# Sorted expert tiles started inside the first stage's tail: 48 of 144 run from a table made at half of the tokens

## What is computed

```python
rw = gating(h2)                                  # [b, t, 16], at most a few experts per token
q = einsum('btc,ech,bte->bth', x2, q_proj, rw)   # k and v alike
attn = softmax(causal(q @ k.T / sqrt(128)))
out = einsum('bth,ehc,bte->btc', attn @ v, o_proj, rw)
return h + attn_linear + out
```

## Time and profile before

| what | value |
|---|---|
| median of 3 runs | 1015.23 us (1014.79 to 1015.39) |
| profiled execution, its own time | 1013.34 us |
| its span | 1011.6 us |
| busy: PE, DVE, ACT, POOL | 928.0, 836.3, 600.6, 632.1 us |
| PE's share of the chain that ended last | 55% (DVE 26%) |
| DMA, mean over the span | 136 GB/s |

### The profile page before, as it was taken

How to read it: one execution, slowest core, us unless ns; L and a number is a source line. 1 busy time by engine, 2 the same in 40 slices (tenths; PEclk the granted TensorE clock), 3 DMA queues, 4 the chain that set the end, 5 groups by cost and what they waited for, 6 DMA issues and landing times.

```text
span 1011.6 us, 20470 instructions
## 1 busy us (share of the span) xinstructions
PE 928.0 (92%) x5230; PEld 800.2 (79%) x5230; DVE 836.3 (83%) x2884; ACT 600.6 (59%) x1633; POOL 632.1 (62%) x832
## 2 busy tenths in 40 slices
PE   4999999999999845999999959999999999999997
PEld 3787788788788734899999938888888888888876
DVE  4789999999999875655555539999999999999998
ACT  4666766666676511644444436666666666666664
POOL 5447777777777678100000058888888888888885
PEclk9999999999999956999999969999999999999999
DMA  2123344443333236898878633333333333333331
GB/s 65 48 74 120 121 142 150 143 146 126 122 125 117 93 109 215 264 298 260 258 248 265 227 116 104 103 104 103 104 104 105 101 105 106 103 105 104 91 105 37
DMA packets 106297, 137.53 MB, mean 136 GB/s; under 512 B 13762, under 2 KB 93634, under 8 KB 106180
## 3 DMA queue, kind: packets, MB, share of 16 engines
q1 hardware_dynamic: 87348, 83.98, 26.7%
q0 software_dynamic: 17408, 50.35, 16.4%
q10 hardware_dynamic: 1424, 1.84, 0.5%
HBM read 70.06 MB, written 66.06 MB: 135 GB/s over the span
## 4 chain that ended last, share of the span: by engine, by line
PE 55%; DVE 26%; POOL 8%; issue 6%; ACT 2%; DMA 2%; SPq 1%; POOLq 0%; DVEq 0%; ACTq 0%
PE bank L1395 15%; PE bank L1396 15%; PE bank L1397 15%; PE bank L1402 5%; DVE phi L1085 4%; DVE attn L1097 2%; DVE kvm L1118 2%; POOL sorted_x L701 2%; DVE stats L1125 2%; POOL row_y L776 2%; DVE stats L970 2%; DVE zden L1094 1%; PE bank L1421 1%; PE bank L1592 1%; PE bank L1598 1%
## 5 line engine op out<-in xcount | busy, mean ns | idle before, releaser
L1395 PE MATMUL bank<-wo_hi,split_lo 128*128 128x512 f32 x512 | 213.7, 417 | 1.5 <-DVE split_lo L1363 1.4
L1396 PE MATMUL bank<-wo_lo,split_hi 128*128 128x512 f32 x512 | 202.8, 396 | 0.0
L1397 PE MATMUL bank<-wo_hi,split_hi 128*128 128x512 f32 x512 | 202.2, 395 | 0.0
L776 POOL DMA_INDIRECT row_y<-sorted_y,pair_now x128 | 131.5, 1027 | 32.1 <-issue 22.9
L769 POOL COPY pair_now<-pair_at 128x2 uint32<-128x2 uint32 x64 | 12.2, 191 | 176.9 <-SPq L574 176.9
L900 ACT ACTIVATE h<-bank,rwo 128x256 f32<-128x256 f32 x256 | 107.2, 472 | 25.0 <-PE bank L1397 15.9
L1234 DVE TENSOR_TENSOR split_lo<-bank,split_hi 128x256 fp32r<-128x256 f32 x144 | 60.8, 422 | 68.6 <-ACT split_hi L861 67.1
L1397 PEld LDWEIGHTS bank<-wo_hi,split_hi 128*128 128x128 f32 x512 | 96.9, 189 | 22.5
L1395 PEld LDWEIGHTS bank<-wo_hi,split_lo 128*128 128x128 f32 x512 | 97.1, 190 | 20.6 <-DVE x L1332 1.6
L1332 DVE SCALAR_TENSOR_TENSOR x<-bank,rwo,x 128x256 f32<-128x256 f32 x256 | 111.1, 474 | 1.1 <-PE bank L1397 1.0
L1332 DVE SCALAR_TENSOR_TENSOR qk_e<-bank,rwo,qk_e 128x256 f32<-128x256 f32 x256 | 110.9, 474 | 0.3 <-PE bank L1397 0.2
(11 more groups left out here) (212 smaller groups left out, 2538.3 us busy)
## 6 DMA issues: line engine op xcount, KB each, us to landing
sorted_y<-row_y SPq DMA_DIRECT2D x36, 384.0 KB, 3.1
sorted_y<-w_attn SPq DMA_DIRECT2D x36, 384.0 KB, 3.2
row_x<-sorted_x SPq DMA_DIRECT2D x72, 128.0 KB, 2.9
h_rows<-h SPq DMA_DIRECT2D x64, 128.0 KB, 1.7
row_x<-h_rows SPq DMA_DIRECT2D x64, 128.0 KB, 3.5
out_h<-row_x SPq DMA_DIRECT2D x64, 128.0 KB, 2.1
phi<-sorted_x SPq DMA_DIRECT2D x36, 128.0 KB, 2.9
qk_neg<-sorted_x SPq DMA_DIRECT2D x36, 128.0 KB, 3.0
```

The costliest lines, as they stand in the source:

```text
L776: pool.indirect_dma_start(out=row_y[:, 2 * tile.p + n, :], out_offset=None, in_=sorted_y, in_offset=offsets(pair_now[tile.q][:, n:n + 1])) ...
L1395: pe.matmul(ps, left[1][c], right[0][c], start=(c == 0), stop=False)
L1396: pe.matmul(ps, left[0][c], right[1][c], start=False, stop=False)
L1397: last = pe.matmul(ps, left[0][c], right[0][c], start=False, stop=(c == n - 1))
```

## The change

The first 48 sorted tiles (`EARLY`) are taken from what is sorted once 32 of the 64 token tiles are ranked. 64 x 128 pairs over 16 experts hold at least 49 full tiles, so 48 full ones are always there. A table of their own (`tab_early`, `early_i`) is formed by DVE in 17 operations, two per step from step 35 on, with a count and two turns by PE added to the rank products. `run1` ends at step 60 for PE, ACT and DVE. Then `run_early` goes through pair tiles -2 to 47; in front of each, `tail(c)` puts the pieces that steps 61 to 67 and the table had. POOL keeps its old steps, and has the late scatters spread otherwise (2, 3, 3, 4, 4, 4, 4 at steps 59, 60, 61, 62, 63, 65, 67, where it had 4, 4, 4, 4, 4, 4 at 59, 60, 61, 63, 65, 67). SP loads tiles 0 to 3 inside the first stage, 4 to 7 behind step 60, and does all 16 fills between tiles 24 and 39. The second table, for the remaining 96 tiles, counts what the first has used. The branch comes behind tile 47.

Buffers: loads of tiles go to `h4` in place of `row_x`; the early tiles' results go to six places (`w_attn` and the raw weight buffers); `ps_y` has three banks in place of four, since one bank holds the tail's products. POOL's shift has 31 pairs of operations, since each expert has two pieces. The pair weights, formed between the tables and the stage before, go in pieces beside tiles 48 to 52, and `routing_part` beside 53 to 57.

```diff
-        ps_turn, ps_y = banks[0:2], banks[2:6]
+        ps_turn, ps_y, ps_dense = banks[0:2], banks[2:5], banks[2:6]
...
+        def run_early(eng, step, tail):
+            for c in range(-2, EARLY):
+                tail(c)
+                step(Tile(c))
...
-            run1(sp, step1)
-            for p in range(2):
-                sp.wait_ge(h2_stored[p], 16 * (B // 2))
-            fill_regions(sp, 0)
-
-            sp.wait_ge(regions_filled, 16 * E)
-            sp.wait_ge(dummies_zeroed, 16 * E)
-            for t in range(B - N_X2, B):
-                scatter_done(sp, t)
+            run1(sp, step1, TAIL_STEP - 3)
+            sp.wait_ge(early_ready, 1)
+            for t in range(EARLY_TOKENS - N_X2, EARLY_TOKENS):
+                scatter_done(sp, t)
+            after(sp, "h2", Tile(B - 5))
+            for c in range(4):
+                load_pair(Tile(c))
+            step1(Tile(TAIL_STEP - 2))
+            step1(Tile(TAIL_STEP - 1))
+            after(sp, "kv_product", Tile(B - 1))
+            after(sp, "qk_exp", Tile(B - 1))
+            for c in range(4, 8):
+                load_pair(Tile(c))
+            step1(Tile(TAIL_STEP))
+
+            for c in range(EARLY):
+                if c == 24:
+                    sp.wait_ge(fill_ready, 1)
+                if 24 <= c < 24 + E:
+                    half, n = divmod(c - 24, E // 2)
+                    if n == 0:
+                        fills.update(enumerate(fill_rows(sp, half)))
+                    sp.dma_start(sorted_x[bass.ds(fills[n], P), :], zeros[:, :]).then_inc(regions_filled, 16)
+                if c + 8 == EARLY:
+                    sp.wait_ge(tables_ready, 1)
+                    sp.wait_ge(regions_filled, 16 * E)
+                    sp.wait_ge(dummies_zeroed, 16 * E)
+                    for t in range(B - N_X2, B):
+                        scatter_done(sp, t)
+                load_pair(Tile(c + 8))
+                if c >= 2 and c % 2 == 0:
+                    store_pair(Tile(c - 2))
+            store_pair(Tile(EARLY - 2))
...
             run1(act, step1)
-            fill_regions(act, 1)
...
+            def tail(k):
+                if k == 2:
+                    attention_formed(Tile(B - 1))
+                    residual_added(Tile(B - 1))
+                    second_stats(Tile(B - 1))
+                    root_inputs(N_ROOTS - 1, Tile(B - 1))
+                if k == 3:
+                    rows_counted(last_group - 2)
+                    experts_chosen(last_group - 1)
...
+                if k == 21:
+                    rows_placed(last_group)
+                if k >= 22:
+                    for n in (2 * (k - 22), 2 * (k - 22) + 1):
+                        if n < N_FINAL_OPS:
+                            final_table(n)
...
+            def tail(k):
+                if k == 1:
+                    sums(last_tile)
+                    logits(Tile(B - 3))
+                if k == 5:
+                    rank(len(GROUPS) - 3)
...
+                if k == 19:
+                    rank(len(GROUPS) - 1)
```

More of the change, by code:

```diff
@@ L533, in step1, with load_pair @@
                     sp.dma_start(h2_rows[tile.t], h2[tile.p][:, :]).then_inc(h2_stored[tile.p], 16)
-            run1(sp, step1)
+            rows, fills = {}, {}
+            def load_pair(tile):
+                if tile.q == 0:
+                    n = tile.c if tile.c < EARLY else tile.c - EARLY
+                    at = (early_i if tile.c < EARLY else tab_i)[0:1, 1, n:n + 4]
+                    loaded = nc.values_load_multi_w_load_instructions(
+                        at, engines=(sp.engine,), min_val=0, max_val=(E * REGION + E * P) - P,
+                        skip_runtime_bounds_check_because="a tile of a region or one of the spare tiles")[1]
+                    rows.update(enumerate(loaded))
+                after(sp, "pair_turned", tile.shift(-8))
+                sp.dma_start(x_buf[tile.c % 8], sorted_x[bass.ds(rows[tile.q], P), :]
+                             ).then_inc(pair_loaded[tile.c % 8], 16)
@@ new lines, in _, with turn_and_product @@
+            experts = {}
+            last_tile = Tile(B - 1)
+            def turn_and_product(i):
+                if i.c >= 0 and i.inside(PAIR_TILES) and i.q == 0:
+                    n = i.c if i.c < EARLY else i.c - EARLY
+                    loaded = nc.values_load_multi_w_load_instructions(
+                        (early_i if i.c < EARLY else tab_i)[0:1, 0, n:n + 4], engines=(pe.engine,), min_val=0,
+                        max_val=E - 1,
+                        skip_runtime_bounds_check_because="the number is limited to E - 1 where it is formed")[1]
+                    experts.update(enumerate(loaded))
+                tile = i.shift(2)
+                if tile.inside(PAIR_TILES):
+                    after(pe, "pair_lo", tile.shift(-2))
+                    pair_landed(pe, tile)
+                    turn(ps_turn[tile.p], *halves(x_buf[tile.c % 8])).then_inc(done["pair_turned"], 1)
+                if i.inside(PAIR_TILES):
+                    e = experts[i.q]
+                    if i.c < len(ps_y):
+                        after(pe, ("v_copied", "phi_q_T", "kv_masked")[i.c], last_tile)
+                    after(pe, "pair_copied", i.shift(-len(ps_y)))
+                    after(pe, "pair_lo", i)
+                    product(ps_y[i.c % len(ps_y)][:, 0:Y], [[w[:, c, :] for c in range(CH)] for w in split[i.q]],
+                            [[w[:, bass.ds(e, 1), c, :].rearrange("p e n -> p (e n)") for c in range(CH)]
+                             for w in wq]).then_inc(done["pair_product"], 1)
```

666 lines of the change are left out of this document (417 added, 249 removed).

## The result

Four runs of the changed kernel have a median of 1004.01 us (1003.18 to 1004.37), four of the kernel before, on the same chip, 1015.01 us. The ratio is 0.989, with a 95% interval of 0.9873 to 0.9907: 11.0 us faster, where 14.8 were forecast. The profiled execution of the change is one of 1004.01 us with a span of 1002.3, so the two profiled spans differ by 9.3 us.

What follows compares the result with a forecast made beforehand. PE was taken to bound the sorted and last stages, DVE the first. -31.5 + 3.0 + 3.7 + 1.5 + 1.5 + 7.0 = -14.8 us gave 998.5 against the profiled 1013.34, set at 1000.4 against the median; range 989 to 1009.

Steps and rivals of the forecast that it cites:

- P(0): Start of the sorted stage's first product: from 392.89 to about 361.4, -31.5 us; 364.4 with the first stage's costs.
- The early table, +3.0: First stage: 17 table operations and two copies out of PSUM on DVE cost +3.0 us, bounds 1.5 and 4.
- Tail pieces +3.7: Early pair tiles: sums, logits, turns, rank pairs and count now stand between PE's products, +3.7 us, bounds 3 and 4.5.
- burst +1.5: After pair tiles 1 and 2: two DVE pieces in a row, 4.1 us, exceed slack and free time; +1.5 us, 0 to 3.
- slow start 1.6: Start of the sorted stage: about a tile and a half at half clock, about 1.6 us, left as before; change 0.
- The branch, +1.5: After tile 47, now in the stream: PE pauses +1.5 us, from 0 if hidden behind queued matmuls to 2.5.
- SyncE, +7.0: Sorted stage: SP's issue falls behind PE, +3.6 us with the fills and +3.4 with the weights; together +7, bounds 0 and 12.
- The last stage, 0: Last stage, after the sorted one: claimed to stay within 1 us of its old length.
- SP keeps up: Rival, 17%: branch and DVE's bursts hide, fills run into the slack; 990.4 us.
- DMA and SP together bind harder: Rival, 13%: late scatters and early pair tiles share DMA engines, landings slow, both crossings cost 5 to 8 us more; 1006 to 1012.
- the clock cost one product: Rival, 6%: PE pausing for DVE in the first tiles keeps half clock, 1.08 us more a tile; 1052 for all 48.
- the tail's end: Rival, 4%: POOL or a piece is held up, tile 48 waits beyond 5 us margin and 6.8 slack; whole gain gone at 27 us.

Runs made afterwards that it cites:

- one wait: The changed kernel, but the second scatter of a token tile waits only for the residual, not again for the tile's positions: 998.39 us, ratio 0.9841 to the kernel before.
- the kernel with three edits: The changed kernel with one wait at the second scatter, all 16 fills through GpSimd and the routing parts behind tiles 76 to 92: 992.88 us, ratio 0.979.

## Why the prediction was right, and where it was not

The result is inside the range and on the forecast side; the median is 3.6 us above the forecast. Point by point:

- **The gain.** "P(0) at about 361.4" but for the first stage's costs: confirmed. With one wait it comes at 364.99, and the forecast had 364.4 with the early table in it.
- **The early table, +3.0.** In the kernel with one wait the starts of `phi` stand 0.83 us behind those of the kernel before at token tile 38 (0.5 of it from its very first tile), 3.25 at 48 and 3.91 at 51, when the last copies are done: 3.1 us.
- **The step that failed** is the sentence "The POOL, ACT and SP work added there has idle time around it." It looked at the idle time of an engine, not at what stands in a ring with it. The added wait cost 3.6 us at P(0) and 1.5 more in the first product's clock, of which 0.8 is left at the last product. With it right, the forecast for the change would have been some 4 to 5 us later, at 1004 to 1005.
- **Tail pieces +3.7, burst +1.5, slow start 1.6.** Together 6.8 for tiles 1 to 32. Measured: 5.7 in the change; 4.2 with one wait, when the clock is up. Oversized by 1.1 to 2.6. The burst by itself is 1.4 at tiles 4 and 5; taking it apart gave back 0.9.
- **The branch, +1.5.** Tile 48 loses 1.0 us in the change, 0.45 with the fills away and nothing that shows in the kernel with three edits. That a slack which is whole covers it is my reading.
- **SyncE, +7.0.** The rate was right: 1.55 us a tile was forecast, and the change has it at 1.51 (four loads with their fills from 420.32 to 426.35). The part for the fills, 3.6, measured 5.1, the wait for the last fill in it. The weights were priced at 4.9, less the 1.4 that they cost before. Tiles 57 to 72 lose 5.5, but 2.6 of it is VectorE's routing parts; the weights have 2.9, and before tiles 18 to 25 lost 2.4, where they were loaded and used. So the net for the weights was 0.5 and not 3.4, and the routing parts, which had no term, cost 2.6 where they had cost 1.2 before, a net 1.4. The total came out at the forecast (5.1 + 0.5 + 1.4 = 7.0) by luck: the fills were too low, the weights far too high, and a fifth of it belongs to another engine. The DMA engines, of which the prediction says "There is no room to catch up in", set no bound there: with the fills elsewhere they moved 312 GB/s over 40 us where the change had 264.
- **The routing parts, no term.** The prediction speaks of "the pair weights" that go "one part a tile into DVE's free time"; the five routing parts behind them it does not mention. They take 1.22 us each, nearly one a tile, against 0.57 us of free time, and this is the second step that failed. I had not looked up their length.
- **The last stage, 0.** It is 2.9 us longer in this pair of profiles, from the last product's start. Over the profiles of kernels that share its code the length from there goes from 431.2 to 434.2: 431.2, 433.4 and 432.7 with the first and second stage of before, 432.1 to 434.2 with those of the change. About 1.4 us of the 2.9 is the pace that goes with the buffers' addresses (6.383 against 6.347 us a tile over 40 tiles), for which the forecast had no term. The rest is within what the length varies by between kernels with the same addresses, and what sets it is open. The operation of 1020 ns goes with none of it (698 ns in a kernel with 433.4).

Of the signs, the waits for loads came where they were forecast, 2.3 us at tiles 38 to 45 and 2.1 at 64 to 70, with 3.8 of waits for VectorE's low halves beside them. Of the rivals, "SP keeps up" did not come about, though at tiles 37 to 48 it nearly does once the fills are elsewhere; "DMA and SP together bind harder" has its mechanism against it, since with slower landings and less issue the kernel became faster; the clock cost one product and did not stay down; the tail's end held nothing up that the trace shows. My tests, a stretch "under 196 or over 212" and P(0) "after 370", stood at 200.8 and 368.6 and so passed a forecast with two missing terms: each looked at a sum.

## What to carry to other kernels

Before costing an added instruction or wait at nothing because its engine has idle time, follow the ring that it stands in over all engines, once round a step, and write down the slack: here 0.40 us in 5.3, and a wait that was already satisfied took 0.50. An idle share of a quarter said nothing of it. When code is rewritten into a flatter loop, compare the waits of each instruction with those of before: here a wait that was logically redundant was not free. And look up the length of every operation that is moved into a stream with little free time; the five of 1.22 us were not in the forecast at all. Where a term is a difference, take the price before from the trace as well: the routing parts and the weights had both cost something in the old place.

## What was not expected of the hardware

- A scatter on GpSimd that waits for two semaphores, one of them long satisfied, starts 0.78 us (0.81 at most) behind the end of the operation that releases it, in each of the seven kernels with two waits; with one wait it is 0.28 us, in the six others.
- A gather on GpSimd takes 1.02 to 1.04 us when it starts 0.12 us or more ahead of VectorE's `wq_lo <- raw,wq_hi` (238 gathers), 1.20 to 1.34 when it starts with it or up to 0.10 behind (166 of 171), and 1.02 to 1.06 again when it starts 0.25 to 0.39 us behind (24).
- `w_attn <- row_y,pair_w,w_attn` on VectorE ends 0.41 to 0.42 us behind the end of the GpSimd operation that runs when it starts, in all but four of 410 cases; its 0.61 to 1.05 us are that wait and this constant.
- The last stage takes 6.347, 6.367 or 6.383 us a token tile, and the figure goes with the placement of the buffers, not with the code ahead of it. An unused buffer of 32 bytes gave back 0.036 us a tile.
- The clock in the first product was full in four kernels and down in six, with the same pause of 2.94 us ahead; down, it cost 0.9 to 1.6 us. The six are those with two waits.
